# Five more unread TensorE products at the head of the image-token kernel: three behind the first group's embedding, one each behind its key tails and receptance tails

## What is computed

```python
h = einsum('bnk,ok->bno', patches(x), W_tok)          # 36 patch tokens, 192 channels
h = concatenate([cls_tok, h], axis=1)                 # 37 tokens per image
a = layernorm(h)
# attention block on a
k, v, sr = ln(a) @ Wk.T, ln(a) @ Wv.T, sigmoid(ln(a) @ Wr.T)
a = a + sr * bi_wkv(decay / 37, first / 37, k, v) @ Wo.T   # scans over the tokens, both ways
a = a + sigmoid(ln(a) @ Wr_f.T) * (square(relu(ln(a) @ Wk_f.T)) @ Wv_f.T)
h = h + a
# 16 experts, 4 of them per token, and a shared one
m = layernorm(h)
h = h + route(m) . (silu(m @ gWg) * (m @ gWu) @ gWd) + silu(m @ sWg) * (m @ sWu) @ sWd
```

## Time and profile before

| | |
|---|---|
| median of 3 executions | 255.41 us (255.34 to 255.53) |
| the profiled execution's own time | 255.63 us |
| its span in the trace | 253.5 us, 4370 instructions |
| TensorE busy (matmul) | 242.6 us, 96% |
| TensorE weight loads | 222.6 us, 88% |
| VectorE busy | 191.4 us, 76% |
| ScalarE busy | 151.0 us, 60% |
| chain that ended last, by engine | TensorE 73%, ScalarE 9%, VectorE 8%, issue 4%, DMA 3% |

### The profile page before, as it was taken

The page is one execution under the profiler, slowest core; times in us unless marked ns, Lnnn a source line. Parts: engine busy times, 40 slices in busy tenths (PEclk is TensorE's granted clock), DMA queues, the critical chain, the costliest instruction groups (busy, mean ns, idle before and its releaser), DMA issues.

```text
span 253.5 us, 4370 instructions
## 1 busy us (share of the span) xinstructions
PE 242.6 (96%) x1508; PEld 222.6 (88%) x1508; DVE 191.4 (76%) x490; ACT 151.0 (60%) x311; POOL 17.9 (7%) x29
## 2 busy tenths in 40 slices
PE   8789899899999999999999999999999999999994
PEld 7677477677588899999999999999999999999993
DVE  5489988999989999999797799877323275843442
ACT  2797899978769999735767862335631341232220
POOL 6100302003101000101100001010000010000000
PEclk9997999999999999999999999999999999999999
DMA  6958271100000430000005510000354000014510
GB/s 170 332 176 309 85 243 62 38 0 0 0 3 10 106 94 13 0 3 0 1 11 157 185 43 1 1 3 0 82 173 136 18 3 0 1 40 92 102 33 27
DMA packets 13165, 17.46 MB, mean 69 GB/s; under 512 B 2359, under 2 KB 11224, under 8 KB 13016
## 3 DMA queue, kind: packets, MB, share of 16 engines
q1 hardware_dynamic: 12872, 17.08, 22.7%
q10 hardware_dynamic: 272, 0.11, 0.2%
HBM read 16.20 MB, written 0.99 MB: 68 GB/s over the span
## 4 chain that ended last, share of the span: by engine, by line
PE 73%; ACT 9%; DVE 8%; issue 4%; DMA 3%; SPq 2%; POOL 0%; DVEq 0%; POOLq 0%
PE PA L998 16%; PE PG L978 16%; PE PG L980 11%; PE PF L998 7%; PE PQ L978 4%; PE PQ L980 3%; PE PX L1029 2%; DMA gates<-c_rows 2%; PE PQ L1049 2%; PE PF L988 1%; PE PG L1149 1%; PE PG L1148 1%; DMA gates<-in_w_k 1%; ACT norm L422 1%; PE PF L1013 1%
## 5 line engine op out<-in xcount | busy, mean ns | idle before, releaser
L584 ACT ACTIVATE act<-PG,columns 128x222 f32<-128x222 f32 (+3 forms) x56 | 28.4, 507 | 58.8 <-PE PG L980 55.1
L978 PE MATMUL PG<-stack,hi_egu 128*128 128x222 f32 (+1 forms) x288 | 62.2, 324 | 0.0
L927 DVE SCALAR_TENSOR_TENSOR hid<-PG,columns,act 128x222 f32<-128x222 f32 (+1 forms) x52 | 27.3, 524 | 28.3 <-PE PG L980 24.8
L998 PE MATMUL PA<-w_ed,hid 128*124 128x192 f32 (+1 forms) x240 | 46.3, 328 | 0.4 <-DVE hid L936 0.3
L978 PEld LDWEIGHTS PG<-stack,hi_egu 128*128 128x128 f32 x288 | 45.6, 190 | 0.7 <-DVE hid L927 0.2
L980 PE MATMUL PG<-stack,lo_egu 128*128 128x222 f32 (+1 forms) x192 | 42.7, 304 | 0.0
L998 PEld LDWEIGHTS PA<-w_ed,hid 128*124 128x124 f32 (+1 forms) x240 | 38.5, 183 | 1.2 <-DVE hid L936 1.2
L980 PEld LDWEIGHTS PG<-stack,lo_egu 128*128 128x128 f32 x192 | 31.8, 190 | 0.0
L396 POOL TENSOR_TENSOR rstd<-var,minus_half 112x2 f32<-112x2 f32 (+3 forms) x12 | 13.9, 1156 | 186.8 <-DVE var L671 186.8
L936 DVE TENSOR_TENSOR hid<-hid,gates 128x222 f32<-128x222 f32 (+1 forms) x48 | 21.9, 462 | 1.8 <-DMA gates<-c_rows 0.9
L998 PE MATMUL PF<-w_down,mix_hid 128*124 128x192 f32 (+1 forms) x120 | 22.8, 326 | 0.0
(11 more groups left out here) (248 smaller groups left out, 443.1 us busy)
## 6 DMA issues: line engine op xcount, KB each, us to landing
gates<-in_w_egu SPq DMA_DIRECT2D x6, 512.0 KB, 4.8
gates<-c_rows SPq DMA_DIRECT2D x16, 138.8 KB, 2.9
gates<-c_rows SPq DMA_DIRECT2D x16, 92.5 KB, 2.8
gates<-c_rows SPq DMA_DIRECT2D x16, 83.2 KB, 2.4
w_ed<-in_w_ed SPq DMA_DIRECT2D x1, 1152.0 KB, 8.0
gates<-c_rows SPq DMA_DIRECT2D x16, 55.5 KB, 2.6
gates<-in_w_up SPq DMA_DIRECT2D x2, 384.0 KB, 4.0
pat<-in_patches SPq DMA_DIRECT2D x2, 370.0 KB, 4.1
```

Source lines behind the costliest of these rows:

```text
L584: nc.scalar.activation(act[128 - gate:128, n % 2, 0:G.n], PG[0:gate, gate_bank(n), 0:G.n], ACT.Silu, bias=bias).then_inc(act_silu, 1)
L927: V_.scalar_tensor_tensor(out, PG[part, 1, 0:G.n], bias, act[part, i, 0:G.n], ALU.add, ALU.mult).then_inc(mul_done, 1)
L978: mm(out, w_hi[:, slot, cols], x[:, p, 0:G.n], start=(p == 0), stop=False, skip_group_check=True)
L998: last = mm(tile_out(P, G, t), src[:, G.ts[t]:G.ts[t] + G.tp], w, start=start and t != 1, stop=stop, skip_group_check=True)
```

## The change

`pe_heat` gets five more spins, none with a wait of its own: `idle0` to `idle2` behind `tok`, and `kt` and `rt` behind `rstd`. `PE_ORDER` puts the first three behind `H:tok`, `H:kt` between `F0:kt` and `F0:v`, and `H:rt` between `F0:rt` and `F0:r`. The rest of the table is the same sequence, with other line breaks.

```diff
             pe.wait_ge(tok_out, 1)
             spin()
             yield "tok"
+            for n in range(3):
+                spin()
+                yield f"idle{n}"
             pe.wait_ge(front_step[0], 1)
             spin()
             yield "stats0"
...
             pe.wait_ge(pool_rstd[1], 1)
             spin()
             yield "rstd"
+            for after in ("kt", "rt"):
+                spin()
+                yield after
             pe.wait_ge(front_step[0], 5)
             spin()
             yield "scan0"
...
 PE_ORDER = _order(
-    "H:early0 H:early1 H:early2 H:early3 H:early4 F0:tok0 H:early5 H:tok H:stats0 H:stats1 H:aggr H:var H:rstd F0:tr1a",
...
+    "H:early0 H:early1 H:early2 H:early3 H:early4 F0:tok0 H:early5 H:tok H:idle0 H:idle1 H:idle2 H:stats0 H:stats1 H:aggr",
+    "H:var H:rstd F0:tr1a F0:tr1b F1:tok0 F1:tok1 F0:k F0:kt H:kt F0:v F0:rt H:rt F0:r H:scan0 H:scan1 H:sb0 H:sb1 H:e1",
...
```

## The result

The change makes the kernel slower. The ratios follow the mean times rather than the medians. In the first comparison the changed kernel took 257.16 us (median of 6 executions, 256.71 to 257.51) and the kernel before 255.43 us; the ratio is 1.0065, with a 95% interval of 1.0051 to 1.0078. In a second comparison, further down, it was 1.0051 (1.0038 to 1.0063), with medians of 256.91 and 255.64 us. So the cost is 1.3 to 1.7 us. The profiled execution took 257.13 us, 1.50 us more than that of before.

What follows compares the result with a forecast made beforehand. VectorE's chain, started by TensorE's transposes, was taken to decide up to group 0's output product at 34.32 us. Terms +1.25, 0 and 0 on the median 255.41 us gave 256.7 us, range 255.9 to 257.6 us.

Steps and rivals of the forecast that it cites:

- The three idle spins: Ahead of the first transposes: 1.28 us of spins, less 0.03 us ScalarE has to spare, delay scan and z: +1.25 us.
- The spins behind kt and rt: Ahead of v and r: both fit in waits for ScalarE, 0.33 and 0.08 us to spare; 0, at most +0.05 us.
- The clock: TensorE's slow stretch, 18.52 to 21.93 us: time won at full clock lies in a wait for VectorE's top; 0.
- What TensorE does up to 34.3 us: From sub0 to the output product: TensorE's work and ScalarE's exponentials stand still while VectorE is 1.25 us late.
- rival 1: Clock falls later, in the waits at 29 to 32 us: total +2.0 us, 257.4 us; chance 0.22.
- the wait for z: Sign: TensorE waits about 1.1 us for z ahead of the output product at 35.57 us.
- The idle time ahead of sub0: Sign: TensorE idle for 0.6 us ahead of sub0 at about 23.25 us if the clock held.
- Rival 2: Waits after 34 us swallow 0.7 to 1.2 us of the delay: 255.4 to 255.9 us; chance 0.13, counted as no change.
- Rival 3: sub0 to sub2 and exponentials: TensorE's products decide, not VectorE; 1.2 us come off, 254.2 us; chance 0.07.
- Rival 4: The two spins don't hold the clock at 18.5 us; still 256.7 us; chance 0.54 together with the forecast.

Runs made afterwards that it cites:

- idle_only: Changed kernel without the spins behind kt and rt, leaving the three idle spins: 256.83 us against 255.64 us for the kernel before, ratio 1.0045.
- idle_in_gap: Changed kernel with the three idle spins moved ahead of the wait for the embedding's copy: 255.68 us against 255.64 us for the kernel before.
- idle_six: Changed kernel with six idle spins in place of three: 258.31 us against 255.61 us for the kernel before, ratio 1.0109.
- tails_only: Changed kernel without the three idle spins, leaving those behind kt and rt: 255.51 us against 255.64 us for the kernel before.
- fewer_norm_spins: Kernel before without its spins var and rstd: 255.66 us against 255.54 us for the kernel before, ratio 1.0004.
- stats_first: Kernel before with VectorE's moments of group 0 ahead of the key weights' low part: 255.95 us against 255.61 us, ratio 1.0017.
- stats_first_tails: Kernel before with group 0's moments ahead of the key weights' low part, plus spins behind kt and rt: 255.78 us against 255.61 us, ratio 1.0010.

## Why the prediction was right

The forecast was 256.7 us, slower, in a range of 255.9 to 257.6 us. The median was 257.16 us in the first comparison; in the second, the increase was 1.27 us and the forecast's +1.25 us.

- **The three idle spins, +1.25 us.** Right in mechanism and in size within 0.03 us. The middle grew by 1.28 us. I had subtracted 0.03 us that ScalarE had to spare at its first copy. The copy did move by only 13.20 - 11.80 - 0.14 = 1.26 us, but the scan and all behind it moved by 1.28 to 1.29 us, so the discount got lost on the way. idle_only, idle_in_gap and idle_six show the three sides of it: these spins alone, elsewhere for nothing, and by their number.
- **The spins behind kt and rt, 0.** Right; tails_only has the middle of before. The waits shrank from 0.61 to 0.17 us ahead of v, and ahead of r none is left.
- **The clock, 0.** Right, and the step on which most hung. The slow stretch went, TensorE came 1.25 us sooner to sub0 (tails_only) and waited there. The first sub product of the changed kernel started at 23.42 us, forecast 23.25 us plus the later head of 0.14 us. The executions of the kernel before with a mean clock of 0.993, which took no longer than the others, say the same.
- **What TensorE does up to 34.3 us** was not quite as forecast. The term for the clock let its work stand still, while the transposes of group 1 moved from 31.36 to 31.93 us with their norm, which the prediction itself counts under rival 1. So the wait for z came out at 0.77 us and not about 1.1 us. The idle time ahead of sub0 was 0.26 us and not 0.6 us; the row counts it from the modelled end of the spins, from their starts it is 23.42 - 20.40 - 2.56 = 0.46 us. Neither decides anything, because z comes last.
- **Rival 1, the clock falling later,** did not happen. The wait ahead of group 1's transposes grew to 0.61 us (forecast 0.67 us), and the output product waited for z. None of the eleven executions of the changed kernel has a mean clock under 0.997. I had counted waits as if they decided alone. In idle_only and fewer_norm_spins they were those of the kernel before, and the clock held in their profiles.
- **Rival 2, swallowed,** did not happen: the wait of 0.7 us in the earlier trace rows is there unchanged, 1.41 us later, and the rest behind the output product is 220.8 to 221.4 us in every kernel.
- **Rival 3, TensorE's products decide,** fell with tails_only.
- **Rival 4** did not occur in a profile of the changed kernel, and its executions' mean clocks give no sign of it.
- What the forecast left out is the head. It took the profile's 8.13 us as fixed, while the head was 8.27 and 8.88 us in two profiles of the changed kernel, by the landing of the key weights, and 8.02 to 8.88 us over all kernels with the same head. The measured median lies 0.5 us above the forecast. Of the 1.73 us of the first comparison 0.45 us are not the 1.28 us of the middle; that they are variation of head and rest is likely from their size and was not shown. That the second comparison meets the forecast within 0.02 us is in part luck for the same reason.

The wait of rows 7 in the changed kernel, from TensorE's timeline (45.27 us before):

```profile
46.68 0.91 PE L1029 MATMUL PX<-w_tok,pat 128*124 128x192 f32 x4 [0.66 <-ACT h L450]
```

## What to carry to other kernels

Filler work keeps an engine busy for free only where it ends before the engine's next input is ready. Placed behind the wait that ends an idle time, it starts when the idle time is over, and costs its full length if the queue is already past its data. Before buying a higher clock, ask which engine the stretch waits for: here 1.25 us of TensorE's time turned into waits for VectorE, and only a much longer slow stretch (6.83 us) reached the end.

## What the runs showed of the hardware that I had not expected

- The granted clock's fall is not a property of the program alone. The kernel before shows a mean of 0.993 in 17 of 94 executions and 0.996 or more in the others. With the same three waits of 0.61, 0.15 and 0.35 us ahead of v, rt and r, the clock fell at 18.5 us in the profile of the kernel before and held in those of idle_only, stats_first and fewer_norm_spins.
- TensorE's first products are slow, and for how long varies. The ten spin entries from 1.10 us took 4.27 us in the kernel before, about twice what later ones take. The embedding's eight products took 1.46 us in nine of the fourteen profiles and 1.70, 1.83, 2.21, 2.22 and 2.35 us in five. It held VectorE's moments back by 0.21 us in idle_six and by 0.51 us in fewer_norm_spins. The granted clock reads 1.00 in all of these stretches, so no trace here shows the clock as the cause.
- GpSimd's power on 112x4 elements takes 1.02 us alone and 1.65 us beside VectorE's two subtractions (stats_first, stats_first_tails). In the eleven profiles with a subtraction beside it, it ends 0.87 to 0.88 us after the last of them. An earlier start of VectorE's work bought nothing as long as the subtractions came with it.
